# Attention and FP4 feed-forward layer in one kernel: quantisation moved to its own buffer and given no due time, the output bias folded into the down weights, row transfers shared with SyncE

## The reference, cut to what matters

```python
def reference(x, w_attn, b_attn, w_proj, b_proj, w_gate, w_up, w_down):
    xn = layernorm(x, eps=1e-5)
    # 16 heads of width 8, S = 2048, causal, mask -log(distance + 1)
    q, k, v = split(xn @ w_attn + b_attn)
    attn = softmax(q @ k.T / sqrt(8) + power_law_mask)     # -inf for keys on one side of the diagonal
    a = (attn @ v) @ w_proj + b_proj
    # every operand of the three products is rounded to FP4 in blocks of 16: scale = max|x| / 6
    gate, up = fp4(xn) @ fp4(w_gate).T, fp4(xn) @ fp4(w_up).T
    f = fp4(silu(gate) * up) @ fp4(w_down).T               # inner width 352
    return x + a + f
```

## Time and profile before

| | before |
|---|---|
| median of 3 runs | 683.89 us |
| profiled execution | 685.19 us |
| its span, first to last instruction | 683.4 us |
| TensorE busy | 587.4 us (86%) |
| VectorE busy | 581.5 us (85%) |
| GpSimd busy | 509.0 us (74%) |
| ScalarE busy | 402.3 us (59%) |
| mean granted TensorE clock | 0.953 |

### The profile page before, as it was taken

How to read it: one execution, slowest core, us unless ns; L and a number is a source line. 1 busy time by engine, 2 the same in 40 slices (tenths; PEclk the granted TensorE clock), 3 DMA queues, 4 the chain that set the end, 5 groups by cost and what they waited for, 6 DMA issues and landing times.

```text
span 683.4 us, 11295 instructions
## 1 busy us (share of the span) xinstructions
PE 587.4 (86%) x3788; PEld 264.4 (39%) x3839; DVE 581.5 (85%) x1206; ACT 402.3 (59%) x857; POOL 509.0 (74%) x386
## 2 busy tenths in 40 slices
PE   6998588668989798989898898989898898987895
PEld 6676354233434342433332342343234343342323
DVE  4786497999899999889999999999997999896462
ACT  3657146254565556566575666658564666667692
POOL 6034337885878887776879898789896798898893
PEclk9999799797999999999999999999998999999997
DMA  4344312201000000110000000000000000000000
GB/s 135 88 135 120 109 31 57 60 4 68 1 2 3 1 0 3 39 47 2 1 1 1 3 17 0 2 2 1 2 1 1 17 1 1 2 2 1 1 2 16
DMA packets 14717, 16.69 MB, mean 24 GB/s; under 512 B 1594, under 2 KB 14171, under 8 KB 14243
## 3 DMA queue, kind: packets, MB, share of 16 engines
q1 hardware_dynamic: 13859, 15.56, 8.2%
q10 hardware_dynamic: 800, 0.40, 0.2%
HBM read 11.75 MB, written 4.01 MB: 23 GB/s over the span
## 4 chain that ended last, share of the span: by engine, by line
PE 43%; POOL 23%; DVE 13%; ACT 8%; issue 7%; DMA 3%; ACTq 2%; SPq 1%; POOLq 0%; DVEq 0%
POOL ring L763 16%; PE psum L1357 10%; PE psum L1315 9%; PE psum L1339 7%; DVE mxp L1098 5%; DMA qop<-parts_dram 3%; ACT ring L915 3%; PE psum L1290 2%; PE psum L1207 2%; POOL xw L781 2%; POOL xw L779 2%; DVE ring L1125 2%; ACTq L927 2%; PE psum L1275 2%; POOL xw L783 2%
## 5 line engine op out<-in xcount | busy, mean ns | idle before, releaser
L763 POOL TENSOR_TENSOR ring<-ring,dist 128x1024 f32<-128x1024 f32 (+3 forms) x209 | 410.6, 1985 | 109.5 <-ACT ring L915 108.7
L1098 DVE TENSOR_REDUCE mxp<-psum 128x1 f32<-128x512 f32 (+3 forms) x640 | 356.3, 599 | 38.3 <-PE psum L1318 18.8
L915 ACT ACTIVATE ring<-psum 128x512 f32<-128x512 f32 (+3 forms) x418 | 199.7, 527 | 133.6 <-PE psum L1342 74.4
L1315 PE MATMUL psum<-kop,qop 96*128 96x512 bf16 (+3 forms) x640 | 205.3, 361 | 19.6 <-DMA qop<-parts_dram 7.4
L1339 PE MATMUL psum<-qop,kop 128*128 128x512 bf16 (+3 forms) x590 | 182.4, 354 | 20.6 <-ACT ring L915 7.9
L1357 PE MATMUL psum<-ring,vaug 128*32 128x512 f32 (+3 forms) x1280 | 154.1, 552 | 17.9 <-POOL ring L763 16.1
L915 ACT ACTIVATE psum<-psum 128x512 f32<-128x512 f32 (+3 forms) x222 | 113.2, 546 | 59.1 <-PE psum L1339 27.6
L1125 DVE TENSOR_TENSOR ring<-psum,dist 128x512 f32<-128x512 f32 (+3 forms) x222 | 133.5, 625 | 15.2 <-ACT psum L915 14.3
L1315 PEld LDWEIGHTS psum<-kop,qop 96*128 96x128 bf16 x640 | 58.3, 99 | 139.5 <-DVE mxp L1098 48.7
L1339 PEld LDWEIGHTS psum<-qop,kop 128*128 128x128 bf16 x640 | 59.9, 99 | 103.9 <-DVE ring L1125 24.0
L1318 PE MATMUL psum<-tri_q,identb 128*128 128x128 bf16 x256 | 57.3, 225 | 0.0
(11 more groups left out here) (132 smaller groups left out, 508.9 us busy)
## 6 DMA issues: line engine op xcount, KB each, us to landing
kop<-parts_dram SPq DMA_DIRECT2D x9, 384.0 KB
qop<-parts_dram SPq DMA_DIRECT2D x9, 384.0 KB
parts_dram<-qpart SPq DMA_DIRECT2D x18, 128.0 KB, 2.9
xin<-_attn_hidden_states_dram SPq DMA_DIRECT2D x4, 256.0 KB, 4.6
ring<-inv_dram SPq DMA_DIRECT2D x1, 1024.0 KB, 5.0
out_dram<-xin SPq DMA_DIRECT2D x4, 256.0 KB, 2.3
qop<-mrow ACTq DMA_DIRECT2D x48, 4.0 KB
parts_dram<-qpart SPq DMA_DIRECT2D x6, 96.0 KB
```

The source lines that it names most:

```text
L763: g_.tensor_tensor(slot(p)[:, :, 0:n], slot(p)[:, :, 0:n], both, ALU.mult).then_inc(weighed_pool, 1)
L915: a_.activation(scores if pair_vec[p] else slot(p)[:, e % 2, 0:n], scores, ACT.Exp, scale=SCALE).then_inc(exp_done, 1)
L1098: v_.tensor_reduce(mxp[:, u % 2, 4 * a + j, c - g:c - g + 1], bank(*o)[:, 0:n], AX_X, ALU.max).then_inc(max_used, 1)
L1315: ins = mm(bank(*o)[:, 0:n], qop[0:K_MAX, u // NQ % 2, h, P * a:P * (a + 1)], kop[0:K_MAX, h, k0:k0 + n], start=True, stop=(c != g))
```

## The change

Six things are changed; the arithmetic of the result stays.

1. **fp4.** The buffer of the pieces is now `qx`, a view of `hT`, which is not used before the feed-forward part. `rest` keeps `qc` alone. The pieces are ordered x, x, weights, weights, x, x (X_PIECES, W_PIECES). They have no due time (`at`) and rank 6.5, between urgent maxima and those beyond the lead. A piece of x is ready when TensorE has transposed its chunk (xnT), the weights at a planned 52 us. As there is one buffer, stage 4 of a piece waits for GpSimd's second instruction of the piece before. GpSimd's three instructions are now three items of the plan.
2. **Output bias.** b_proj is loaded as row 96 of `wdT[:, 2]`, and row 96 of `hT[:, :, 2]` is set to 1 after the last piece, so the third product of "down" has 97 rows and the fourth one (L1293) goes.
3. **Rows of maxima.** The transfers of units 0 to 4 stay with ScalarE, those of units 5 to 15 are issued by SyncE.
4. **SyncE's list** after the setup is now planned: loads of q, rows and stores of the output, sorted by planned time.
5. **Split of the weighing.** POOL_QUEUE goes from 2600 to 3800 ns, and to LAST_QUEUE = 1500 once all maxima are done.
6. **Planned durations**: pv longer by 310 columns (129 ns), rows on TensorE 6 x 128 columns instead of 4 x 128, "minor" 740 ns instead of 900, rows on ScalarE 560 ns plus 3 x 620 for its own transfers instead of 1318 ns, the landing of later rows 4500 ns instead of 6000, GpSimd's part of fp4 1345 + 1345 + 1015 ns instead of 3900.

```diff
-PIECES = [(S, WHALF), (S + WHALF, WHALF)] + [(S - GQ * (k + 1), GQ) for k in range(NG)]
+W_PIECES = [2, 3]
+X_PIECES = [0, 1, 4, 5]
+PIECES = {n: (S + WHALF * k, WHALF) for k, n in enumerate(W_PIECES)}
+PIECES.update({n: (S - GQ * (k + 1), GQ) for k, n in enumerate(X_PIECES)})
...
-FP4_AT, FP4_GAP = 80, 10
+FP4_RANK = 6.5
...
-POOL_QUEUE = 2600
+POOL_QUEUE, LAST_QUEUE = 3800, 1500
...
-            needs = [("DVE", ("fp4", n, k - 1))] if k else [("POOL", ("fp4", n - 2))] if n >= 2 else []
-            needs += [("POOL", ("split", 2 * NG - 1, 1))] if n == 0 else [("PE", ("xnT", n - 2))] if n >= 2 else []
-            vec(("fp4", n, k), (GQ, 64, 64, GQ, GQ, GQ)[k], needs, at=FP4_AT + FP4_GAP * n, rank=3)
-        pool(("fp4", n), 3900, [("DVE", ("fp4", n, FP4_STAGES - 1))], rank=1)
+            needs = [("DVE", ("fp4", n, k - 1))] if k else [
+                ("PE", ("xnT", X_PIECES.index(n))) if n in X_PIECES else ("DMA", ("weights",))]
+            needs += [("POOL", ("fp4", n - 1, 1))] if k == 4 and n else []
+            vec(("fp4", n, k), (GQ, 64, 150, GQ, GQ, GQ)[k], needs, rank=FP4_RANK)
+        for k in range(3):
+            pool(("fp4", n, k), (1345, 1345, 1015)[k],
+                 [("POOL", ("fp4", n, k - 1)) if k else ("DVE", ("fp4", n, FP4_STAGES - 1))], rank=1)
...
-        act(("rows", u), GQ / 2, [("PE", ("rows", u))] + ([("DMA", ("rows", u - MROWS))] if u >= MROWS else []), n=5, rank=0)
+        pool(("minor", u), 740, [("DVE", ("parts", u, 1))], rank=0)
+        pe(("rows", u), 6 * P, [("POOL", ("minor", u))], rank=0)
+        add("ACT", ("rows", u), ROWS_COPY + (PARTS * ROWS_ISSUE if u < ROWS_BY_ACT else 0), 0,
+            [("PE", ("rows", u))] + ([("DMA", ("rows", u - MROWS))] if u >= MROWS else []), rank=0)
...
-        pe(("pv", s), 4 * P * blocks[s], needs, rank=5)
+        pe(("pv", s), 4 * P * blocks[s] + PV_SWITCH, needs, rank=5)
...
-                pair_vec[p] = behind > POOL_QUEUE
+                pair_vec[p] = behind > (LAST_QUEUE if work["max"] == total else POOL_QUEUE)
...
+    orders["SP"] = [o for _, o in sorted(late)]
...
+        qx = hT[:].rearrange("p a m n -> p (a m n)")
...
+            for o in orders["SP"]:
+                if o[0] == "q":
+                    gi = o[1]
+                    last = (NQ * (gi - 2) + NQ - 1, TPG * GROUPS[gi - 2])
                     sp.wait_ge(st_psum, 4 * step_no[last] + 4)
+                    load_q(sp, gi, 0, NH, qop_loaded[GROUPS[gi]])
+                if o[0] == "rows":
+                    sp.wait_ge(mT_ready, o[1] + 1)
+                    load_rows(sp, o[1])
+                if o[0] == "out":
...
                 if k == 4:
+                    if n:
+                        vec.wait_ge(fp4_seq, 2 * n)
                     ins = v_.tensor_scalar(c.bitcast(I32), v.bitcast(I32), EXPONENT, None, ALU.bitwise_and)
...
-                    for m, (_, k) in enumerate(FCH):
-                        mm(down_of(i), hT[0:k, i % 2, m], wdT[0:k, m], start=(m == 0), stop=False)
                     if i == 0:
                         pe.wait_ge(late_loaded, 16 * 2)
-                    mm(down_of(i), ones[:], brow[:], start=False, stop=True).then_inc(down_psum, 1)
+                        pe.wait_ge(hones_ready, 1)
+                    for m, (_, k) in enumerate(FCH):
+                        k += m == 2
+                        ins = mm(down_of(i), hT[0:k, i % 2, m], wdT[0:k, m], start=(m == 0), stop=(m == 2))
+                    ins.then_inc(down_psum, 1)
```

More of the change, by code:

```diff
@@ L62 @@
 SEEN = 60
+PV_SWITCH = 310
+ROWS_COPY, ROWS_ISSUE = 560, 620
 PE_COL, PE_DRAIN = 1 / 2.4, 165
@@ L175, in plan @@
             vec(("parts", u, k), 64, needs, rank=0)
-        pool(("minor", u), 900, [("DVE", ("parts", u, 1))], rank=0)
-        pe(("rows", u), 4 * P, [("POOL", ("minor", u))], rank=0)
-        act(("rows", u), GQ / 2, [("PE", ("rows", u))] + ([("DMA", ("rows", u - MROWS))] if u >= MROWS else []), n=5, rank=0)
+        pool(("minor", u), 740, [("DVE", ("parts", u, 1))], rank=0)
+        pe(("rows", u), 6 * P, [("POOL", ("minor", u))], rank=0)
+        add("ACT", ("rows", u), ROWS_COPY + (PARTS * ROWS_ISSUE if u < ROWS_BY_ACT else 0), 0,
+            [("PE", ("rows", u))] + ([("DMA", ("rows", u - MROWS))] if u >= MROWS else []), rank=0)
     for e in range(4 * len(steps)):
@@ L222, in plan @@
         act(("hT", i), 192, [("PE", ("hT", i))] + ([("PE", ("down", i - 2))] if i >= 2 else []), n=2, rank=1)
-        pe(("down", i), 16 * P, [("ACT", ("hT", i))], rank=1)
+        pe(("down", i), 12 * P, [("ACT", ("hT", i))], rank=1)
         vec(("sum", i), P, [("PE", ("down", i))], rank=1)
@@ L243, in plan @@
     seen[("DMA", ("hankel",))] = 25000
+    seen[("DMA", ("weights",))] = 52000
     pair_vec, weighed_by = {}, {}
+    late = []
+    left_out = [TPG + 1] * NG
     bank_of, prior = {}, {}
@@ L349, in take @@
         if kind == "rows" and engine == "ACT":
-            seen[("DMA", item)] = end + DMA_ROWS
+            seen[("DMA", item)] = end + (DMA_ROWS if item[1] < ROWS_BY_ACT else DMA_LATE_ROWS)
+            if item[1] >= ROWS_BY_ACT:
+                late.append((end, item))
         if item == ("rest", 1, 1):
@@ L367, in take @@
                 seen[("DMA", ("q", u // NQ + 2))] = end + 9000
+                late.append((end, ("q", u // NQ + 2)))
+        if kind in ("add", "sum"):
+            left_out[item[1] if kind == "add" else item[1] // TPG] -= 1
+            if left_out[item[1] if kind == "add" else item[1] // TPG] == 0:
+                late.append((end + OUT_SLACK, ("out", item[1] if kind == "add" else item[1] // TPG)))
         orders[engine].append(item)
@@ L480, in build @@
         fsc = sb("fsc", [P, F // BLK], F32)
-        qc = [sb(f"qc{i}", [P, WHALF], F32) for i in range(2)]
+        qc = [sb(f"qc{i}", [P, GQ], F32) for i in range(2)]
         hankel = ring_flat[:, 0:S]
@@ L620, in load_q, with load_rows @@
                              part_i.to_broadcast([PARTS, HD, (h1 - h0) * GQ])).then_inc(signal, 16)
+        def load_rows(queue, u):
+            hq = parts_of(u)[1]
+            for i in range(PARTS):
+                queue.dma_start(qop[MROW + i:MROW + i + 1, u // NQ % 2, 4 * hq:4 * hq + 4, :],
+                                mrow[4 * i:4 * i + 4, u % MROWS, :]).then_inc(mrow_loaded[u % MROWS], 16)
         def slot(p):
@@ L707, in _ @@
                                  pattern=[[-1, P]], channel_multiplier=1).then_inc(consts_ready, 1)
-            g_.memset(ones[:], 1.0).then_inc(consts_ready, 1)
-            pool.wait_ge(consts_ready, 3)
+            pool.wait_ge(consts_ready, 2)
             for i in range(PARTS):
@@ L923, in _ @@
                                   ACT.Identity).then_inc(mT_ready, 1)
-                    hq = parts_of(u)[1]
-                    act.wait_ge(mT_ready, u + 1)
-                    for i in range(PARTS):
-                        act.dma_start(qop[MROW + i:MROW + i + 1, u // NQ % 2, 4 * hq:4 * hq + 4, :],
-                                      mrow[4 * i:4 * i + 4, u % MROWS, :]).then_inc(mrow_loaded[u % MROWS], 16)
+                    if u < ROWS_BY_ACT:
+                        act.wait_ge(mT_ready, u + 1)
+                        load_rows(act, u)
                 if o[0] == "turn":
```

76 lines of the change are left out of this document (39 added, 37 removed).

## The result

| | before | after |
|---|---|---|
| median of 4 runs | 683.3 us | 627.3 us |
| lowest to highest | 682.3 to 686.5 | 626.4 to 627.9 |
| ratio of the runs, 95% interval | | 0.917 (0.914 to 0.921) |
| span of the profiled execution | 683.4 us | 624.5 us |
| TensorE / VectorE busy | 587.4 / 581.5 us | 564.4 / 562.8 us |

The account below looks back on a forecast made before the run. VectorE was taken to bound 115 to 160 us, three near-full engines 160 to 620. fp4 -9, rows -5, bias -5, split 0, end -2, durations 0 sum to -21 from 685.2: 664 us, range 650 to 681.

Parts of the forecast that it names:

- The bound of the stage from 115 to 160 us: VectorE bounds this stage; moving fp4 earlier makes it 34 us instead of 45: -11, bounds 0 and -14.4.
- "+2" for the setup: Before 78 us, fp4's GpSimd instructions and one-buffer wait delay other setup work: +2 us, bounds 0 and +6.
- setup pays for fp4: Rival, chance 0.15: fp4 beside setup work the 21.3 us transfer waits for earns 1 us instead of 9: 672 us.
- Rows, "-5": ScalarE's issues of rows, 11.8 us on the chain in six units, discounted to -5 us; bounds 0 and -11.8.
- Bias, "-5": Dropping the fourth "down" product, 6.4 us on the chain over 15 pieces: -5 us, bounds -3 and -6.5.
- Split of the weighing and planned durations, "0" and "0": Pairs moving to GpSimd from 160 to 620 us: 0, bounds -10 and +14; truer durations only shift order: 0.
- theory T: Theory for the follow-up runs: fp4 gains by TensorE's clock and earlier first pv, the rest because GpSimd no longer idles.
- The end, "-2": From 647 us, LAST_QUEUE gives GpSimd's pairs to VectorE: -2 us, bounds 0 and -3.
- A saving is given back in part: Long stage, 160 to 620 us: the chain spreads over all engines, so one engine's saving partly goes to the next.
- GpSimd becomes the bound: Rival, chance 0.08: from 160 to 620 us too many pairs move to GpSimd, deciding from the 33rd: 694 us.
- All of it passes through: Rival, chance 0.06: TensorE reaches 94% instead of 90% from 160 to 620 us, another 18 us: 646 us.
- signs listed: Profile signs for or against the forecast: fp4 timing, TensorE's share and clock, ScalarE gaps, VectorE's heads, GpSimd above 92%.

Follow-up runs that it names:

- fp4 alone: The kernel before with only the fp4 part changed (own buffer, new piece order, no due time, rank 6.5): ratio 0.980 to before.
- the kernel of 654.4 us: The kernel after, re-planned with ScalarE issuing all transfers of rows, as before: 654.4 us, ratio 0.953 to before.
- meaningless shift: The kernel after with one planner constant moved, only orders shifting: SEEN 64, SEEN 56 or FFN_AT 152; ratios to before 0.932, 0.926, 0.929.
- SEEN 56: The kernel after with an item planned as seen by other engines 56 ns after its end instead of 60: ratio 0.926 to before.
- late fp4: The kernel after with the six fp4 pieces back at their old due times and rank 3: 653.95 us, ratio 0.952 to before.

## Why the prediction was right and wrong

**The bound of the stage from 115 to 160 us: right in place, wrong in price.** That fp4 on VectorE held it is shown by the run with fp4 alone; without it TensorE and VectorE are about equally full there (42.3 and 42.1 of 45 us). The first step that failed is "the stage is 34 us instead of 45: -11 us", with its bound of -14.4 from TensorE's 30.6 us. Those 30.6 us were busy time at a granted clock of 0.83, and there was no reason to take them as the work that the stage could hold: relieved, TensorE does 335 matmuls there instead of 194, at clock 1.00. By the fourth unit fp4 alone is worth some 23 us at equal work, not 11, and at the end 14, not 9. A part of it comes before the stage: the first pv starts at 78.7 us instead of 90.1. It is planned behind the fill, whose last transpose starts at 78.5 instead of 89.9. The forecast did not reckon with the fill; that it alone held the pv up is not shown, since no run has less of it in the kernel before. Nor does a run part what the higher clock gave from what the freed VectorE gave.

**"+2" for the setup: about right.** The first product of the second group, which the 21.3 us transfer let start at 77.2 us in before, starts at 79.9 us with fp4 alone and at 78.3 in after: 2.7 and 1.1 us later. (VectorE's fp4 itself costs 25.4 us instead of 27.3, which is another matter.) One of the meetings, in the timeline of VectorE and then of GpSimd in after:

```profile
73.14 2.36 DVE L1045 TENSOR_SCALAR sc<-amax 128x32 f32<-128x32 f32 x1
```
```profile
73.11 2.35 POOL L802 TENSOR_TENSOR ring<-ring,dist 128x1024 f32<-128x1024 f32 x1
```

The small operation, else 0.17 us long, takes as long as GpSimd's pair and ends with it. The Trainium skill (SBUF — State Buffer, Who interferes with whom) has the shared port pair held for a whole instruction, and the trace agrees. This meeting lies on the chain: TensorE waits 2.33 us, until 75.9 us, for the maximum that stands behind the small operation on VectorE. But the meetings did not decide the time: the rival "setup pays for fp4", 672, fell.

**Rows, "-5": right in the old order, too small in the new one.** 4.4 us measured with before's order, 13 with after's, about the whole bound of 11.8. "Of the others I take a third" was thus right for one order only. What the runs have in common is for whom the order was planned: in the two orders planned for ScalarE's issues (that of before and that of the kernel of 654.4 us) taking them away brings 4 us and nothing, and in the order planned without them putting them back costs 13. That this is the reason was not tested by itself.

**Bias, "-5", bounds -3 and -6.5: too small.** 9.3 us in before's order, 7 in after's. The 6.4 us that stood on the chain was taken as the most it could bring. The 32 instructions took 8.2 us in all. The interval of the 9.3 us, 6.3 to 12.3, leaves out the 5 but not the 6.4, so it is not settled whether the gain is more than the share of the chain.

**Split of the weighing and planned durations, "0" and "0": these two steps failed most.** Each had been put at nothing because both signs seemed open. Taken back together they are worth 19 us, some 11 more than the 8 of a meaningless shift. The pairs that moved were close to the ten of the forecast (14). The sentence that failed is "TensorE stays at 90% and a pair comes back to it later": it did not stay there (93% in the long stage), and with the two parts taken back TensorE is at 91% there and VectorE's extra 18.8 us stand against 19 us of time. That fits a long stage in which a us taken from VectorE goes through because GpSimd has the room. It is not shown: the same re-planning shifts the order, a shift alone costs 8, and with SEEN 56 VectorE is busy 4.6 us less than in after and the kernel is 6 us slower. How the 19 us divide, and how much of them is order, is open. Nor does theory T's last part, GpSimd's idle time, hold as a cause. With GpSimd's work the same (223 pairs, order kept, ScalarE issuing) it rises by 12 us as the time rises by 13: it shows that the time grew, not why.

**The end, "-2".** From the last reduction of maxima to the end it is 62 us in after and 62 with the old queue limits (60 in before). No gain of LAST_QUEUE is to be seen there.

**"A saving is given back in part".** This discount was drawn from a chain spread over all engines. Of fp4's early 23 us some 17 reach the end, a discount of a quarter; the rows were discounted rightly in one order and wrongly in the other, the bias wrongly. Taken back one at a time, the five parts cost 24 + 24 + 19 + 7 + 7 = 81 us, more than the 56 gained together. That each part is worth more when the others are there (fp4 14 us on before and 24 on after) would explain it. So would the order: after is 6 to 10 us better than three of its neighbours, each of the five runs plans anew, and five times 8 us is more than the 25 in excess. The runs do not part the two. On the side of before the parts sum to 14 (fp4 alone, planned anew) + 4 + 9 (rows and bias, orders kept) = 27 us, where the forecast had 19. The other 29 of the 56 us belong to the split, the durations, the end and the order, for which it had 2. There lies most of the miss of 37 us; 1.9 us of it is that the forecast started from the profiled execution, 685.2 and not 683.3.

**The rivals.** "GpSimd becomes the bound" came true in its place (94% busy, head of the chain at 25%) and false in its sign. It was to decide from the 33rd moved pair, and 14 moved. "All of it passes through", 646 at a chance of 0.06, named the right stage and 94% for TensorE (93% measured), and was still 19 us short. Of the signs listed, all that spoke for the forecast came true (the first piece before 50 us and five done at 81, TensorE above 85%, clock near 1, no issue of rows on ScalarE after unit 4, 120 heads on VectorE from 160 to 560 us), so they did not tell 664 from 627; the one listed against it, GpSimd above 92% with TensorE waiting for it, came true too, in a faster kernel. TensorE does wait for L802, 14.1 us in all, but it had waited 16.1 for L763 before. "Fp4 still behind 100 us" came true for GpSimd's part, whose last instruction of fp4 starts at 106.8 us.

**What stays open.** Why an order planned with ScalarE's issues is 24 to 27 us slower whoever issues; how the 29 us that fp4 alone, rows and bias leave over divide between the split, the durations and the order; how much of the last 10 us of after is luck. Neither the split nor the durations were tried on the kernel before, and no run moves pairs to GpSimd with the rest of the order kept.

## What to carry to other kernels

The busy time of a starved engine is no estimate of what its stage will need: look at its clock in that stage, and at how much work it does per us where nothing starves it. In a kernel with planned orders, a parameter that seems only to describe the plan (a duration, a queue limit) can be worth as much as removed work, and a term is priced cleanly only with the orders kept as they are, and even then it has one price in each order (4 and 13 us for the rows); a difference under 10 us between two plans is shown to mean something only beside shifts without meaning. When two kernels are compared at a milestone, compare the work done at it as well: 30.5 us ahead at the fourth unit were 23 at equal work. Three engines above 83% do not by themselves mean that savings are given back; here they hardly were where work moved to the engine with room, though the runs do not show that this is why.

## What the runs showed of the hardware

With VectorE relieved of fp4, TensorE's granted clock in the stage from 115 to 160 us was 1.00 (fp4 alone, and after) instead of 0.83, and with late fp4 it was 0.74. Its mean over the run went from 0.953 to 0.985. A VectorE operation on 128 x 32 values took 2.36 us instead of 0.17 beside one instruction of GpSimd of 2.35 us. And three small transfers issued by ScalarE cost 13 us over eleven units in one order and 4.4 in another, though each issue takes 0.58 us in both (at the median).
